# Attention weights and V multiplied in f32 on four column tiles instead of as f16 parts

## The chip, the cores and the metric

The kernel runs on one core of one Trainium2 chip. The metric is the device time of one execution in microseconds (us); less is better. The engines are PE (TensorE, with its weight loads shown as PEld), DVE (VectorE), ACT (ScalarE), POOL (GpSimd) and SP (SyncE), which issues the DMAs.

## The reference

A decoder block over 32 sequences of 128 tokens with 256 features, all in f32, cut here to its course:

```python
def mha(q_in, k_in, v_in, wq, wk, wv, wo, mask):          # 16 heads of 16 features
    q, k, v = (heads(a @ w + b) for a, w, b in ...)
    scores = einsum('bhqd,bhkd->bhqk', q, k) / 4
    scores = where(mask == 0, -1e9, scores)
    w = softmax(scores, axis=-1)
    out = einsum('bhqk,bhkd->bhqd', w, v)
    return merge(out) @ wo + bo

h0 = layernorm(x)
h1 = ln(h0 + mha(h0, h0, h0, ..., tgt_mask))              # stage A
h2 = ln(h1 + mha(h1, ctx, ctx, ..., src_mask))            # stage B
h3 = ln(h2 + relu(h2 @ w1 + b1) @ w2 + b2)                # stage C
x1 = x + tanh(g_xattn) * h3
out = x1 + tanh(g_ffn) * bitlinear_ffn(layernorm(x1))     # stage E
```

bitlinear_ffn quantizes its activations to 8 bits and its weights to three values, and is a gated network of inner width 1024.

## The kernel before

The 32 sequences go in 16 groups of two (G = 2). The five stages A, B, C, E (A and B have a part that projects, Ap and Bp) are software pipelined: in one turn of the loop, stage A works on one group, B on the group before it, and so on. The first five turns and the last ones are unrolled, the others are one hardware loop (Fori). A **unit** is one stage and one sequence; a turn has four, numbered k = 0, 1 (stage A) and 2, 3 (stage B), and -1 is the last unit of the turn before. What each engine does in a turn, and in which order, is the list SCHEDULE (lines 96 to 117), written by hand. Every engine walks through the same list and issues, in program order, its own part of each step; semaphores tie the parts together. BANK_OF (119 to 127) says which of the four PSUM banks lin_A, lin_B, lin_C and lin_E a step's result goes to.

To keep the accuracy of f32 on f16 matmuls, nearly every operand is held as two f16 tensors, a high part (the value rounded) and a low part (what is left), and a product is three matmuls: high by high, high by low, low by high (`products`, line 583). ACT writes the high part, and DVE or POOL subtracts it for the low part.

Attention of a unit goes through these steps:
- `in` and the DMAs of `parts_out`: Q and K of a group go out to DRAM (parts_AQ, ...) and come back ordered by head (stk_AQ, stk_AK, stk_BQ, stk_BK).
- `smax` (L655, L659): PE makes the scores with the queries on partitions, four heads at a time, into the bank smax. DVE takes each row's maximum (nm, L1119; L1126 and L1128 split it in two f16 parts), step `M` turns it (L669, PE), ACT copies it (mT) and a DMA puts it into two spare rows of stk_.Q.
- `scores` (L680, L685): PE makes the scores again, with the keys on partitions and the maximum already taken off, 8 heads (half a unit, hf) at a time, into the 1024 columns of st. ACT takes the exponential twice, to f32 (e32, L894) and to f16 (ehi, L896), and POOL subtracts: elo = e32 - ehi (L1283).
- `values` (lines 687 to 705): the weights are the stationary operand, V moves past them. For each of 8 heads three matmuls, of 17, 16 and 17 columns, go into the bank av, which ends with the queries on partitions. V is in vhi and vlo; vhi has a 17th column per head, a constant, which gives the sum of the weights. DVE takes the reciprocal of the sums (L1136) and multiplies (o, L1138). `values` of hf 1 is the second half.
- `O` (L714): PE turns o in two f32 transposes; ACT writes the high part oT (L905), DVE the low part (L1143).
- `W` (L593, L583): PE projects; DVE adds the residual and takes the statistics (L1150, L1037 to L1046); POOL takes the power -0.5 (lrs, L1268).
- `N`: DVE normalizes (L1051), POOL multiplies by the gain and adds the bias (L1290, L1298).

Other steps that stand around the change: `Ap` or `Bp` with `T`, `X` (transposes), `K`, `Q`, `V` (projections, each with two bias matmuls and 12 products; V's high part is written by ACT at L866, its low part vlo by DVE at L1105); `C` with `F` and `F2` (the feed forward of stage C), `stats` and `apply`; `E` with `norm` (DVE's norm and scales of the last network, then ACT at L836), `TQ` (L619), `GU` (L742), `Q2` and `DN` (L748, L752), and `setup`, once-only work on the three-valued weights in the first turns.

The order at one place of the list:

```python
    ("scores", 0, 0), ("values", -1, 1), ("Bp", "K"), ("smax", 1, 1), ("Bp", "V"), ("Bp", "T"), ("O", -1),
    ("E", "norm"), ("W", -1), ("smax", 1, 2), ("in", "B", "K"), ("N", -1), ("Bp", "Q"), ("E", "TQ"),
```

## Time and profile before

| what | value |
|---|---|
| three runs | 1305.58, 1314.23 and 1314.6 us, median 1314.23 |
| span of the profiled execution, first to last instruction | 1305.9 us (no time around it is given for this execution; its span is that of the lowest run) |
| mean granted clock of PE, of full speed | 0.880 |
| PE busy | 941.4 us (72%), 10103 matmuls |
| PEld busy (beside PE) | 737.1 us (56%) |
| DVE busy | 902.5 us (69%) |
| ACT busy | 561.7 us (43%) |
| POOL busy | 549.1 us (42%) |
| DMA | 38.2% of 16 engines' span |

How to read it: busy time counts an engine's instructions, overlaps once. A matmul's length is that of one instruction from start to end; matmuls follow each other faster than that, so what one costs in a row is the distance between starts. In rows ordered in time, a start (us from the span's start) and a length stand first, "xN" says that N instructions are merged, and the bracket is the time the engine sat idle before them and what ended it. 128*32 ahead of a shape is the part of the array that the weights fill.

### The profile page before, as it was taken

How to read it: one execution, taken by the hardware profiler on the slowest of the kernel's cores; microseconds unless marked ns; L12 is line 12 of the kernel's file. 1: busy time of each engine (PE TensorE's matmuls, PEld its weight loads, DVE VectorE, ACT ScalarE, POOL GpSimd, SP SyncE). 2: the span in 40 equal slices, each digit the busy share in tenths (PEclk: the TensorE clock that was granted, in tenths of full speed). 3: DMA queues.
4: the chain of work that ended last, by engine and by line, in shares of the span. 5: the costliest groups of instructions: out<-in, count | busy, mean ns of one | idle time of the engine just before them, and what ended most of it. 6: DMA issues, size and time to landing. Idle time of an engine off the chain costs nothing.

```text
span 1305.9 us, 28843 instructions
## 1 busy us (share of the span) xinstructions
PE 941.4 (72%) x10103; PEld 737.1 (56%) x10147; DVE 902.5 (69%) x2063; ACT 561.7 (43%) x836; POOL 549.1 (42%) x468
## 2 busy tenths in 40 slices
PE   1254567868778787878787778797878778786674
PEld 1133445646666665656665657575756666564452
DVE  8544356558787877787878788686868787666544
ACT  2212243435444554545455445453535454542432
POOL 5012134453535454444536354535453545460510
PEclk9866677979898989898999999898999898988886
DMA  4523442424444444453544425243534444404000
GB/s 139 121 81 49 78 55 42 84 40 77 64 74 75 73 73 73 57 89 53 93 53 78 64 68 75 54 81 55 86 48 76 65 65 74 66 10 66 17 9 8
DMA packets 136288, 85.07 MB, mean 65 GB/s; under 512 B 10632, under 2 KB 131631, under 8 KB 136240
## 3 DMA queue, kind: packets, MB, share of 16 engines
q1 hardware_dynamic: 136240, 84.43, 38.2%
q8 instruction: 31, 0.51, 0.2%
q14 instruction: 17, 0.14, 0.1%
...
## 4 chain that ended last, share of the span: by engine, by line
PE 27%; DVE 21%; DMA 18%; issue 16%; POOL 10%; ACT 4%; SPq 3%; DVEq 1%; POOLq 0%; ACTq 0%
DMA stk_AQ<-parts_AQ 9%; PE lin_A L583 4%; PE lin_E L583 3%; DMA parts_AQ<-qk_AQ 3%; DMA stk_BQ<-parts_BQ 3%; PE lin_B L583 3%; PE smax L659 3%; SPq L476 3%; POOL lrs L1268 2%; DVE nm_A L1119 2%; PE smax L655 2%; PE st L685 2%; DMA parts_BQ<-qk_BQ 2%; PE lin_B L752 2%; DMA stk_AQ<-mT_A 2%
## 5 line engine op out<-in xcount | busy, mean ns | idle before, releaser
L1283 POOL TENSOR_TENSOR elo<-e,ehi 128x1024 f16<-128x1024 f32 x128 | 272.6, 2130 | 303.4 <-ACT ehi L896 302.8
L894 ACT ACTIVATE e<-st 128x1024 f32<-128x1024 f32 x128 | 131.0, 1024 | 190.5 <-PE st L685 190.4
L1268 POOL TENSOR_TENSOR lrs<-lve,neghalf 128x1 f32<-128x1 f32 (+1 forms) x112 | 70.0, 625 | 333.8 <-DVE lve L1046 332.2
L1119 DVE TENSOR_REDUCE nm_A<-smax 128x4 f32<-128x512 f32 x128 | 87.8, 686 | 81.3 <-PE smax L659 80.9
L896 ACT ACTIVATE ehi<-st 128x1024 f16<-128x1024 f32 x128 | 130.9, 1022 | 0.0
L655 PE MATMUL smax<-mb,ident_big 128*128 128x512 f16 x128 | 57.6, 450 | 101.5 <-DMA stk_AQ<-parts_AQ 73.7
L1119 DVE TENSOR_REDUCE nm_B<-smax 128x4 f32<-128x512 f32 x128 | 87.7, 685 | 20.1 <-PE smax L659 19.8
L659 PE MATMUL smax<-stk_BK,stk_BQ 126*128 126x128 f16 x512 | 51.7, 225 | 45.2 <-DMA stk_BQ<-parts_BQ 40.9
L655 PEld LDWEIGHTS smax<-mb,ident_big 128*128 128x128 f16 x128 | 13.2, 103 | 112.8 <-issue 54.2
L659 PEld LDWEIGHTS smax<-stk_BK,stk_BQ 126*128 126x128 f16 x512 | 35.1, 100 | 60.3 <-issue 24.7
L875 ACT ACTIVATE late<-late,magic_col,s 128x1024 f32<-128x1024 f32 x32 | 39.7, 1240 | 60.8 <-DVE s L1195 60.8
L680 PE MATMUL st<-mbT,ident_big 128*128 128x512 f16 x128 | 54.0, 422 | 6.0 <-DMA stk_AQ<-mT_A 5.1
L659 PEld LDWEIGHTS smax<-stk_AK,stk_AQ 126*128 126x128 f16 x512 | 45.9, 110 | 21.7 <-issue 10.4
L659 PE MATMUL smax<-stk_AK,stk_AQ 126*128 126x128 f16 x512 | 57.9, 243 | 0.0
L836 ACT ACTIVATE late<-late,magic_col,s 128x256 f32<-128x256 f32 x32 | 17.5, 592 | 90.5 <-DVE kap L1080 90.5
L685 PEld LDWEIGHTS st<-stk_AQ,stk_AK 128*128 128x128 f16 x512 | 43.2, 106 | 21.3 <-issue 7.4
L685 PE MATMUL st<-stk_AQ,stk_AK 128*128 128x128 f16 x512 | 53.6, 231 | 0.0
L583 PE MATMUL lin_E<-hT_C,w 128*128 128x256 f16 x384 | 50.6, 272 | 0.0
L619 PE MATMUL lin_E<-ident,late 128*128 128x128 f32 x64 | 12.2, 321 | 51.2 <-ACT late L836 51.2
L699 PE MATMUL av<-vhi_B,ehi 128*128 128x17 f16 x512 | 45.6, 172 | 3.0 <-POOL elo L1283 3.0
L1051 DVE TENSOR_SCALAR h<-x_a,lmv,lrs 128x256 f32<-128x256 f32 x32 | 37.4, 1209 | 14.5 <-POOL lrs L1268 14.5
L685 PE MATMUL st<-stk_BQ,stk_BK 128*128 128x128 f16 x512 | 44.5, 237 | 2.6 <-DVE mw L1011 1.3
...
## 6 DMA issues: line engine op xcount, KB each, us to landing
...
```

The costliest lines, as they stand in the source:

```text
L583: mm = eng.matmul(dst, lhs(a, k), rhs(b, k), start=(start and at == 0), stop=(at == last))
L655: eng.matmul(smax[:, :], ident_big[:, :], mb[:, :].unsqueeze(1).to_broadcast([P, 4, P]), start=True, stop=True)
L659: mm = eng.matmul(smax[:, i * P:(i + 1) * P], stk[s, "Q"][0:XROW, h, tok], stk[s, "K"][0:XROW, h, tok], start=(s == "B"), stop=True, skip_ ...
L680: eng.matmul(st[:, k2 * 512:(k2 + 1) * 512], ident_big[:, :], mbT[:, :].unsqueeze(1).to_broadcast([P, 4, P]), start=True, stop=True)
L685: mm = eng.matmul(st[:, col:col + P], stk[s, "K"][:, h, tok], stk[s, "Q"][:, h, tok], start=(s == "B"), stop=True, skip_group_check=True)
L699: eng.matmul(dst, ehi[:, hf, i * P:(i + 1) * P], vhi[s][:, b, h, :], start=True, stop=False, skip_group_check=True)
L875: eng.activation(q2m[:, :], z2[:, :], ACT.Identity, scale=s2[:, 0:1], bias=magic_col[:, 0:1]).then_inc(q2_ready, 1)
L894: eng.activation(e32[:, hf, :], st[:, :], ACT.Exp, scale=SCORE).then_inc(e32_ready, 1)
L896: eng.activation(ehi[:, hf, :], st[:, :], ACT.Exp, scale=SCORE).then_inc(st_drained, 1)
L1119: eng.tensor_reduce(nm[s][:, 4 * part:4 * part + 4], smax[:, :].rearrange("p (h k) -> p h k", h=4), AX_X, ALU.max, negate=True).then_inc(s ...
L1268: eng.tensor_tensor(lrs[n][:, a:b], lve[n][:, a:b], neghalf[:, 0:b - a], ALU.pow).then_inc(ln_rstd[n], 1)
L1283: eng.tensor_tensor(elo[:, hf, :], e32[:, hf, :], ehi[:, hf, :], ALU.subtract).then_inc(elo_ready, 1)
```

## The change

V is held in one f32 tensor v32, 32 columns a head: 16 of V, and 16 of the constant. ACT writes it straight from PSUM, and DVE's subtraction is gone. The exponential is taken once, to f32 (e32); ehi, elo and POOL's subtraction are gone, and so are their semaphores. In `values` the operands change places: v32 of a head (128x32) is stationary and the weights of that head (128x128, f32) move past it. Head h = 4c + j writes partitions 32j to 32j+31 of columns 128c to 128c+127 of av: one f32 matmul a head, four heads on the four column tiles of the array. av thus holds the values with the features on partitions. ACT copies av to SBUF (av_sb) when both halves are done. A new step `R` turns av_sb back with four f32 transposes into a lin bank, and DVE's reciprocal and product read that bank. In the list, `R` of a unit stands where `O` stood or near it, `O` where `W` stood or later, and W -1, N -1, W 0 and C T move back.

```diff
-VA = DH + 1
+VA = 2 * DH
...
-    ("scores", 0, 0), ("values", -1, 1), ("Bp", "K"), ("smax", 1, 1), ("Bp", "V"), ("Bp", "T"), ("O", -1),
-    ("E", "norm"), ("W", -1), ("smax", 1, 2), ("in", "B", "K"), ("N", -1), ("Bp", "Q"), ("E", "TQ"),
...
+    ("scores", 0, 0), ("values", -1, 1), ("Bp", "K"), ("smax", 1, 1), ("Bp", "V"), ("Bp", "T"), ("R", -1),
+    ("E", "norm"), ("O", -1), ("smax", 1, 2), ("in", "B", "K"), ("Bp", "Q"), ("E", "TQ"),
...
-    plain = {"A": ("T", "K", "V"), "B": ("X", "V", "T", "Q"), "C": ("T",)}[stage]
+    plain = {"A": ("T", "K"), "B": ("X", "T", "Q"), "C": ("T",)}[stage]
...
-        vlo = {s: sb(f"vlo_{s}", [P, G, NH, DH], F16) for s in "AB"}
+        v32 = {s: sb(f"v32_{s}", [P, G, NH, VA], F32) for s in "AB"}
         nm = {s: sb(f"nm_{s}", [P, NH], F32) for s in "AB"}
         nm2 = {s: sb(f"nm2_{s}", [P, 2 * NH], F16) for s in "AB"}
         mT = {s: sb(f"mT_{s}", [2 * NH, P], F16) for s in "AB"}
         e32 = sb("e32", [P, 2, 1024], F32)
-        ehi = sb("ehi", [P, 2, 1024], F16)
-        elo = sb("elo", [P, 2, 1024], F16)
+        av_sb = sb("av_sb", [P, 512], F32)
         rsum = sb("rsum", [P, NH], F32)
         o = {s: sb(f"o_{s}", [P, NH, DH], F32) for s in "AB"}
...
                 for i in range(8):
                     h = 8 * hf + i
-                    dst = av[:, h * VA:h * VA + VA]
-                    eng.matmul(dst, ehi[:, hf, i * P:(i + 1) * P], vhi[s][:, b, h, :], start=True, stop=False,
-                               skip_group_check=True)
-                    eng.matmul(av[:, h * VA:h * VA + DH], ehi[:, hf, i * P:(i + 1) * P], vlo[s][:, b, h, :],
-                               start=False, stop=False, skip_group_check=True)
-                    mm = eng.matmul(dst, elo[:, hf, i * P:(i + 1) * P], vhi[s][:, b, h, :], start=False, stop=True,
-                                    skip_group_check=True)
+                    c, j = h // 4, h % 4
+                    mm = eng.matmul(av[VA * j:VA * (j + 1), c * P:(c + 1) * P], v32[s][:, b, h, :],
+                                    e32[:, hf, i * P:(i + 1) * P], start=True, stop=True)
                 mm.then_inc(av_filled, 1)
+
+            def rows_back(st_, k):
+
+                s, b, g, turn = st_.unit(k)
+                bank, fill, drain, before, after = st_.job(s, ("R", k))
+                wait(eng, drain, before)
+                eng.wait_ge(av_drained, turn.at(1, 1))
+                for c in range(4):
+                    mm = eng.transpose(bank[:, c * P:(c + 1) * P], av_sb[:, c * P:(c + 1) * P], ident[:, :])
+                mm.then_inc(fill, 1)
 
             def output_rows(st_, k):
 
...
+                eng.wait_ge(*st_.read(s, ("R", k)))
                 for c in range(DC):
                     mm = eng.transpose(bank[:, c * P:(c + 1) * P],
...
                 elif name == "V":
-                    dst = vhi[s][:, :, :, 0:DH].rearrange("p b h d -> p (b h) d")
+                    dst = v32[s][:, :, :, 0:DH].rearrange("p b h d -> p (b h) d")
                     src = bank[:, :].rearrange("p (n d) -> p n d", d=DH)
+                    eng.activation(dst, src, func).then_inc(drain, 1)
+                    return
...
                 if what == "scores":
                     eng.wait_ge(st_filled, turn.at(2, hf + 1))
-                    wait(eng, elo_ready, turn.at(2, hf - 1))
-                    eng.activation(e32[:, hf, :], st[:, :], ACT.Exp, scale=SCORE).then_inc(e32_ready, 1)
                     wait(eng, av_filled, turn.at(2, hf - 1))
-                    eng.activation(ehi[:, hf, :], st[:, :], ACT.Exp, scale=SCORE).then_inc(st_drained, 1)
+                    eng.activation(e32[:, hf, :], st[:, :], ACT.Exp, scale=SCORE).then_inc(st_drained, 1)
+                elif what == "values":
+                    if hf == 0:
+                        return
+                    eng.wait_ge(av_filled, turn.at(2, 2))
+                    wait(eng, sums_ready, turn.at(1))
+                    eng.activation(av_sb[:, :], av[:, :], ACT.Copy).then_inc(av_drained, 1)
                 elif what == "M":
...
-                    i_ = eng.tensor_tensor(vlo[s][:, :, :, :].rearrange("p b h d -> p (b h) d"),
-                                           bank[:, :].rearrange("p (n d) -> p n d", d=DH),
-                                           vhi[s][:, :, :, 0:DH].rearrange("p b h d -> p (b h) d"), ALU.subtract)
                 else:
...
                     eng.scalar_tensor_tensor(nm2[s][:, NH:2 * NH], nm[s][:, :], 1.0 / MS, nm2[s][:, 0:NH], ALU.mult,
                                              ALU.subtract).then_inc(max_ready[s], 1)
-                elif what == "values":
-
-                    if part == 0:
-                        return
-                    eng.wait_ge(av_filled, turn.at(2, 2))
-                    heads = av[:, 0:NH * VA].rearrange("p (h v) -> p h v", v=VA)
+                elif what == "R":
+
+                    bank, fill, drain, before, after = st_.job(s, ("R", k))
+                    eng.wait_ge(fill, after)
+                    heads = bank[:, :].rearrange("p (h v) -> p h v", v=VA)
                     eng.reciprocal(rsum[:, :], heads[:, :, DH]).then_inc(sums_ready, 1)
                     eng.wait_ge(sums_ready, turn.at(1, 1))
                     eng.tensor_tensor(o[s][:, :, :], heads[:, :, 0:DH], rsum[:, :].unsqueeze(2).to_broadcast([P, NH, DH]),
-                                      ALU.mult).then_inc(av_drained, 1)
+                                      ALU.mult).then_inc(drain, 1)
                 elif what == "O":
...
 
-                const(eng.memset(vhi[s][:, :, :, DH:VA].rearrange("p b h o -> p (b h o)"), WS))
+                const(eng.memset(v32[s][:, :, :, DH:VA].rearrange("p b h o -> p (b h) o"), WS))
             assert n_const[0] == N_CONST
...
             def unit_step(st_, what, k, hf=0):
                 s, b, g, turn = st_.unit(k)
                 n = LN_OF[s]
-                if what == "scores":
-                    eng.wait_ge(st_drained, turn.at(2, hf + 1))
-                    wait(eng, av_filled, turn.at(2, hf - 1))
-                    eng.tensor_tensor(elo[:, hf, :], e32[:, hf, :], ehi[:, hf, :], ALU.subtract).then_inc(elo_ready, 1)
-                elif what == "W":
```

The steps as PE issues them, at the turn's start, behind V and T of stage B: lin_E<-ident,o_B is O -1, brows and w_BO are W -1, w_BQ is Bp Q. Before:

```order
L583 MATMUL lin_C<-w_BV,hT_B 128x256 x12
L613 MATMUL lin_A<-ident,h 128x128 x4
L714 MATMUL lin_E<-ident,o_B 128x128 x2
L593 MATMUL lin_E<-brows,ones 128x256
L583 MATMUL lin_E<-w_BO,oT_B 128x256 x6
L655 MATMUL smax<-mb,ident_big 128x512
L659 MATMUL smax<-stk_AK,stk_AQ 128x128 x4
L591 MATMUL lin_B<-ones,brows 128x256
L583 MATMUL lin_B<-hT_B,w_BQ 128x256 x6
```

The same place on PE, now:

```order
L581 MATMUL lin_C<-w_BV,hT_B 128x256 x12
L611 MATMUL lin_A<-ident,h 128x128 x4
L708 MATMUL lin_B<-ident,av_sb 128x128 x4
L718 MATMUL lin_E<-ident,o_B 128x128 x2
L653 MATMUL smax<-mb,ident_big 128x512
L657 MATMUL smax<-stk_AK,stk_AQ 128x128 x4
L589 MATMUL lin_B<-ones,brows 128x256
L581 MATMUL lin_B<-hT_B,w_BQ 128x256 x6
...
L591 MATMUL lin_E<-brows,ones 128x256
L581 MATMUL lin_E<-w_BO,oT_B 128x256 x6
```

R -1 (av_sb) has come in, directly ahead of O -1, and W -1 has moved behind B's Q and two smax steps.

Further on, still on PE, where stage A's K and Q are projected: brows with w_AO is W 0, nm_B is M 2, w_AK and w_AQ are the projections. Before:

```order
L703 MATMUL av<-vhi_A,elo 128x17
L593 MATMUL lin_E<-brows,ones 128x256
L583 MATMUL lin_E<-w_AO,oT_A 128x256 x6
L669 MATMUL lin_C<-ident,nm_B 32x128
L659 MATMUL smax<-stk_BK,stk_BQ 128x128 x4
L591 MATMUL lin_A<-ones,brows 128x256
L583 MATMUL lin_A<-hT_A,w_AK 128x256 x6
```

The same place on PE, now:

```order
L718 MATMUL lin_C<-ident,o_A 128x128 x2
L667 MATMUL lin_C<-ident,nm_B 32x128
L657 MATMUL smax<-stk_BK,stk_BQ 128x128 x4
L589 MATMUL lin_A<-ones,brows 128x256
L581 MATMUL lin_A<-hT_A,w_AK 128x256 x6
...
L581 MATMUL lin_B<-hT_A,w_AQ 128x256 x6
L591 MATMUL lin_E<-brows,ones 128x256
L581 MATMUL lin_E<-w_AO,oT_A 128x256 x6
```

W 0 stood ahead of K and Q and stands behind them now; O 0 is where W 0 was.

On DVE, at the turn's start ahead of stage E's norm (lst<-late): rsum and o_B are the reciprocal and product, oT_B is O -1's low part. Before:

```order
L1119 TENSOR_REDUCE nm_A<-smax 128x4
L1136 RECIPROCAL rsum<-av 128x16
L1138 TENSOR_TENSOR o_B<-av,rsum 128x256
L1099 TENSOR_TENSOR qf_B<-lin_A,anyb 128x512
L1119 TENSOR_REDUCE nm_A<-smax 128x4
L1105 TENSOR_TENSOR vlo_B<-lin_C,vhi_B 128x512
L1090 TENSOR_TENSOR hT_B<-lin_A,hT_B 128x512
L1143 TENSOR_TENSOR oT_B<-lin_E,oT_B 128x256
L1037 BN_STATS lst<-late 128x6 x2
```

The same place on DVE, now:

```order
L1131 TENSOR_REDUCE nm_A<-smax 128x4
L1115 TENSOR_TENSOR qf_B<-lin_A,anyb 128x512
L1131 TENSOR_REDUCE nm_A<-smax 128x4
L1106 TENSOR_TENSOR hT_B<-lin_A,hT_B 128x512
L1147 RECIPROCAL rsum<-lin_B 128x16
L1149 TENSOR_TENSOR o_B<-lin_B,rsum 128x256
L1051 BN_STATS lst<-late 128x6 x2
```

The reciprocal and product have moved behind hT_B's low part, vlo_B is gone, and oT_B's low part comes after stage E's norm.

## Rows read from the trace of the kernel before

**Rows 1.** Stretches: us, then PE, PEld, DVE, ACT, POOL busy; clock, DMA, GB/s

```profile
0.00:300.00 300.00, 157.45 (x1503) 118.21 (x1505) 166.42 (x316) 86.56 (x123) 99.64 (x87) 0.77 0.40 77
300.00:1100.00 800.00, 646.48 (x7347) 516.42 (x7382) 615.82 (x1453) 395.23 (x596) 380.86 (x321) 0.93 0.43 69
...
800.00:813.60 13.60, 13.55 (x167) 11.45 (x166) 11.75 (x32) 9.13 (x13) 7.19 (x7) 1.00 0.65 91
744.30:813.60 69.30, 55.03 (x628) 43.40 (x631) 53.99 (x126) 33.86 (x51) 33.09 (x29) 0.95 0.43 69
```

**Rows 2.** PE in order of time: start us, length us, engine, line

```profile
749.26 0.60 PE L655 MATMUL smax<-mb,ident_big 128*128 128x512 f16 x1 [4.71 <-DMA stk_AQ<-parts_AQ]
...
753.25 0.38 PE L655 MATMUL smax<-mb,ident_big 128*128 128x512 f16 x1
```

**Rows 3.** The chain that ended last, from 800 us on: start, length

```profile
806.15 2.87 DMA parts_AQ<-qk_AQ
...
810.38 8.28 DMA stk_AQ<-parts_AQ
```

**Rows 4.** PE's waits from 744.3 to 813.6: us in total, times, longest

```profile
PE smax L655 <- DMA stk_AQ<-parts_AQ: 4.7, 1, 4.7
PE lin_E L619 <- ACT late L836: 2.5, 1, 2.5
PE lin_E L593 <- DVE oT_B L1143: 1.8, 1, 1.8
PE smax L655 <- DVE nm_A L1119: 1.7, 1, 1.7
PE smax L659 <- DMA stk_BQ<-parts_BQ: 1.2, 1, 1.2
PE lin_C L669 <- DVE nm_A L1128: 1.1, 1, 1.1
```

**Rows 5.** PE in order of time: a values block, and around L669

```profile
743.52 0.18 PE L699 MATMUL av<-vhi_B,ehi 128*128 128x17 f16 x1
...
744.14 0.42 PE L714 MATMUL lin_A<-ident,o_A 128*128 128x128 f32 x2
...
812.74 0.23 PE L669 MATMUL lin_B<-ident,nm_B 128*32 128x128 f16 x1
812.90 0.18 PE L699 MATMUL av<-vhi_B,ehi 128*128 128x17 f16 x1
```

**Rows 6.** PE in order of time, the set-up and the first projection

```profile
24.58 2.08 PE L554 MATMUL lin_E<-late,bvb 128*128 128x256 f32 x4
...
44.64 1.49 PE L583 MATMUL lin_A<-hT_A,w_AK 128*128 128x256 f16 x6
```

**Rows 7.** PE in order of time, f32 transposes and f16 scores

```profile
803.71 0.62 PE L748 MATMUL lin_A<-ident,late 128*128 128x128 f32 x4
804.20 0.66 PE L748 MATMUL lin_B<-ident,late 128*128 128x128 f32 x4
...
805.24 0.61 PE L685 MATMUL st<-stk_BQ,stk_BK 128*128 128x128 f16 x8
```

**Rows 8.** Groups: busy us, mean ns of one, idle before and its end

```profile
L1283 POOL TENSOR_TENSOR elo<-e,ehi 128x1024 f16<-128x1024 f32 x128 | 272.6, 2130 | 303.4 <-ACT ehi L896 302.8
L896 ACT ACTIVATE ehi<-st 128x1024 f16<-128x1024 f32 x128 | 130.9, 1022 | 0.0
L1051 DVE TENSOR_SCALAR h<-x_a,lmv,lrs 128x256 f32<-128x256 f32 x32 | 37.4, 1209 | 14.5 <-POOL lrs L1268 14.5
L1051 DVE TENSOR_SCALAR late<-late,lmv,lrs 128x256 f32<-128x256 f32 x64 | 29.9, 509 | 14.2 <-POOL lrs L1268 14.2
L1138 DVE TENSOR_TENSOR o_B<-av,rsum 128x256 f32<-128x256 f32 x32 | 13.6, 425 | 1.1
```

**Rows 9.** DVE and POOL in order of time, one place

```profile
759.86 1.59 DVE L1126 TENSOR_SCALAR nm_A<-nm_A 128x16 f16<-128x16 f32 x1
...
759.30 2.12 POOL L1283 TENSOR_TENSOR elo<-e,ehi 128x1024 f16<-128x1024 f32 x1
```

More of the change, by code:

```diff
@@ L105 @@
     ("scores", 1, 0), ("smax", 2, 1), ("E", "GU", 0, 3), ("values", 0, 1), ("E", "GU", 1, 0), ("smax", 2, 2),
[2 rows of a table removed]
[2 rows of a table added]
     ("setup", 0), ("E", "GU", 1, 2), ("E", "DN", 0, 0), ("E", "DN", 0, 1), ("N", 0), ("E", "GU", 1, 3),
     ("scores", 2, 0), ("smax", 3, 2), ("values", 1, 1), ("in", "A", "Q"), ("E", "Q2", 1), ("setup", 1),
[1 row of a table removed]
[1 row of a table added]
     ("C", "stats"), ("O", 1), ("smax", 4, 0), ("E", "DN", 0, 2), ("setup", 2), ("W", 1),
-    ("scores", 3, 0), ("smax", 4, 1), ("values", 2, 1), ("N", 1), ("E", "DN", 1, 0), ("smax", 4, 2),
[1 row of a table added]
     ("E", "DN", 1, 1), ("O", 2), ("scores", 3, 1), ("smax", 4, 3), ("E", "DN", 1, 2), ("W", 2), ("M", 4),
@@ L159, in job_of @@
         return None
-    if step[0] in ("M", "O", "W"):
+    if step[0] in ("M", "R", "O", "W"):
         return unit_of(t, step[1])[0], step
@@ L711, in output_rows @@
                 wait(eng, drain, before)
-                eng.wait_ge(av_drained, turn.at(1, 1))
+                eng.wait_ge(*st_.read(s, ("R", k)))
                 for c in range(DC):
@@ L914, in iteration @@
                         continue
-                    if what in ("scores", "M", "O"):
+                    if what in ("scores", "values", "M", "O"):
                         unit_step(st_, *step)
+                    elif what in ("R",):
+                        continue
                     elif name in ("GU", "DN", "Q2"):
@@ L1212, in iteration @@
                         continue
-                    if what in ("smax", "values", "O", "W", "N"):
+                    if what in ("smax", "R", "O", "W", "N"):
                         unit_step(st_, *step)
+                    elif what == "values":
+                        continue
                     elif step == ("Ap", "norm"):
```

13 lines of the change are left out of this document (8 added, 5 removed), and 9 rows, old and new, of the table SCHEDULE.

## Prediction

> **What bounds the kernel now.** I read the page first (its busy shares are in the table above: TensorE, PE, 72%, VectorE, DVE, 69%, nothing full), then the table of stretches, PE's waits, the groups, and last the rows in order of time. The stretches [rows 1] show that the page's average mixes two kinds of time: PE is busy 157 of the first 300 us (filling the pipeline, once-only weight work), but 646 of the 800 us from 300 to 1100, which is the loop; the last 206 us drain it. PE waits for stk_AQ at 749.26 [rows 2], and the next turn's load of it lands at 810.38 + 8.28 = 818.7 [rows 3], so a turn takes about 69.3 us and the middle holds 800 / 69.3 = 11.5 of them. The list of PE's waits in the turn from 744.3 to 813.6 [rows 4] has 4.7 + 2.5 + 1.8 + 1.7 + 1.2 + 1.1 = 13.0 us, and smaller ones of 1.0. PE is thus occupied 69.3 - 14.0 = 55.3 us; it is the fullest engine, and it waits for the answers of other engines to its own results: a chain through DRAM, and layer norms on DVE and GpSimd (POOL). More PE work is paid for in full outside such a chain and costs nothing beside one. So I work out a turn from both: PE's work, and each wait anew.
>
> **The values step carries the answer.** Before, half a unit is 24 f16 matmuls of 17 or 16 columns: the first starts at 743.52, the next step (L714) at 744.14 [rows 5], 0.62 us. There are 128 such blocks, 8 a turn. After, a block is 8 f32 matmuls that move 128 columns, each into its own quarter of the output partitions.
>
> What an f32 matmul costs, the set-up shows. L554 issues two of 256 columns, and the row has four instructions in 2.08 us [rows 6]: two per matmul, (2.08 - 0.63) / 3 = 0.48 apart, 0.63 being the length of one. The f16 matmuls of 256 columns at 44.64 are about (1.49 - 0.42) / 5 = 0.21 apart [rows 6]. Where the granted clock is 1.00 [rows 1], a f16 matmul of 128 columns takes (0.61 - 0.23) / 7 = 0.054 us [rows 7], a quarter of 0.21 for half the columns. The early rows thus ran at the lower of the two levels, and there an f32 instruction cost about two f16 passes, an f32 matmul four. At the upper level a new matmul is 4 x 0.054 = 0.22 us, and eight in a row are 1.74 us. What the four column tiles can do side by side no row shows: the one matmul on a narrow tile, L669 (128*32), always stands alone.
>
> The bounds are 1.74 / 4 = 0.44 us, all tiles at once, and 1.74, none beside another. I take a value between: the two instructions of a matmul use one tile, so the second cannot stream while the first does, and if instructions start in order, only the second of one head overlaps the first of the next. The queue then moves on by 0.11 a matmul: 8 x 0.11 + 0.11 = 1.0 us.
>
> To this comes a change of tile size at both ends. After L669 at 812.74 the next matmul starts 0.16 later [rows 5], not 0.054: 0.1 us. Taken twice a block, 0.2 (nothing, if that gap was a wait). The block becomes 1.2 us, +0.58, with ends +0.02 (no overlap lost, with the changes) and +1.3.
>
> The Trainium skill, page TensorEngine Tiling (Array Packing), Key Properties, says that different tiles can load weights and multiply in parallel, but that changing the tiling mode drains the engine. By its first half the block would be the 0.44 us of full overlap, by its second that change is owed at every block, which speaks against the edit; the 0.16 us behind L669 agrees with the second half, and no run here shows the first.
>
> **The other parts, per turn of four units.**
> - R, four f32 transposes a unit. L748 has the shape: one set of four starts at 803.71, the next at 804.20 [rows 7], some 0.45 each. +1.8 us.
> - ScalarE (ACT) loses L896, 1.02 us x 8 [rows 8], and gains one 128x512 f32 copy a unit, between nothing seen and that 1.02. It was busy 33.9 of 69.3 [rows 1], so nothing comes of it by itself.
> - POOL loses elo, 2.13 us x 8 [rows 8]. It stood in front of the values, but is not among PE's waits [rows 4]: the old order hides it already.
> - DVE loses vlo and gains more in another way. While elo runs, DVE's tensor_scalar from SBUF to SBUF stands still: L1126, 16 columns, takes 1.59 us at 759.86, beside an elo from 759.30 to 761.42 [rows 9]. L1051 writing h averages 1.21 us, the same shape writing late 0.51 [rows 8]; 0.7 x 2 a turn, L1126 twice, and the nrm groups between: about 3 us of DVE a turn. Worth nothing where DVE is not waited for, all 3 at most.
> - Clock: behind the wait of 4.7 us L655 takes 0.60 instead of the 0.38 it takes four us later [rows 2], so some 4 us of PE work run at the lower level and cost 2. A wait half as long gives back about 1.
>
> PE's work: 55.3 + 8 x 0.58 + 1.8 - 1.0 = 60.7 us.
>
> **Each wait anew [rows 4].**
> - stk_AQ, 4.7: its chain (DVE, ACT, POOL, DMAs of 2.87 and 8.28 [rows 3]) stays. PE's work beside it grows by two blocks (1.2), R 1 (0.45) and W 0, which now follows Q instead of preceding K (seven matmuls of 256 columns, 14 x 0.054 = 0.76). 2.3 are left.
> - oT_B, 1.8, ahead of W -1: goes with W's move, but O -1 now follows R -1 at once and needs DVE's reciprocal and product (L1138 0.42 [rows 8], about 0.7 together), behind hT_B's low part. Queued behind O -1 on PE are smax and B's Q. 2.1.
> - ACT late L836, 2.5: PE comes to it as before (O -1 starts where W -1 did), but DVE starts that norm behind o_B instead of oT_B, 0.4 later. 2.9.
> - nm_A, 1.7 + 1.1: L1126's stall sits in it. 1.2.
> - stk_BQ, 1.2: W -1 and a block are now beside it. 0.
> - The small ones 1.0, and 0.6 for R 2, which has only four transposes between it and O 2.
> Sum 10.1; 60.7 + 10.1 = 70.8. Of DVE's 3 us I count 1.2 on the way, the part in the norms that PE waits for: 69.6 us a turn, against 69.3. Over 11.5 turns +4 us. At both ends PE is half idle and units run by their latency. There a half unit loses 1.02 + 2.13 us ahead of its values and gains up to 1.3: I take 8 us less in all, of 0 to 20. For the profiled execution that is 1305.9 + 4 - 8 = 1302 us. Of the three runs before, one (1305.6) is at its span and two are at 1314, with 8 us more at the median; I add half of that: **1306 us**, about no change (this measurement tells some 1% from none).
>
> **Rivals.**
> 1. *The tiles do not overlap* (slower). Block 1.74 + 0.2 = 1.9 us, +1.3. PE: 55.3 + 10.4 + 1.8 - 1.5 = 66.0; waits: stk_AQ 0.9, the rest as above, 8.7; less 1.2: 73.5. +4.2 x 11.5 - 4 = +44: 1350, and +10 at the ends, where passes at the lower level take twice as long: 1360. It decides from a block of 1.3 us up. For it: two instructions per matmul, and no row with an overlap. Against it: no row excludes one.
> 2. *Four tiles at once* (faster). Block 0.64; PE 55.3 + 0.2 + 1.8 - 0.3 = 57.0; waits 3.5 + 2.1 + 2.9 + 1.2 + 0.4 + 1.6 = 11.7; less 1.2: 67.5. -1.8 x 11.5 - 10 = -31: 1278. For it: the four heads of a group share nothing. Against it: both instructions of a head on one tile.
> 3. *Each change from one tile to another costs the 0.1 us of L669*, not only the change of size: 8 x (0.22 + 0.1) = 2.6 us a block, +2.0, 16 us of PE a turn. Some 7 fall into waits: +9 x 11.5 = 104: 1415.
> 4. *DVE's relief counts in full*, with the middle block: 1.8 us a turn more, 21 us, and 10 more at the ends: 1275. For it: L1126 and L1051 are in chains that PE waits for. Against it: DVE waits for PE as well.
>
> **How the numbers follow.** Middle case 0.35 (own range 1290 to 1325: faster by over 1% 0.08, within 0.22, slower 0.05), no overlap 0.25 (slower), four at once 0.21 (faster 0.18, same 0.03), full relief 0.13 (faster), a price per tile 0.06 (slower). Faster 0.39, same 0.25, slower 0.36. The range leaves out the last case and the outer ends of the others: 1262 to 1378.
>
> **What would show it.** In the changed kernel's profile: from the first values matmul to the next step's first 1.2 us (rivals 0.64, 1.9, 2.6), and a head's second instruction starting with the next head's first. L1051 on h near 0.5 us. PE's wait for stk_AQ near 2.3. A turn of 69.6 us. A block over 1.3 us with a turn of 69 or less would prove my reading of the waits wrong; a block of 1.2 and a turn near 67, the value I put on DVE's relief.

## The result, and the profile after it

| | before | changed kernel |
|---|---|---|
| median of four runs each | 1314.41 us | 1423.24 us (1419.59 to 1432.34) |
| span of the profiled execution | 1305.9 us | 1417.8 us |
| mean granted clock of PE | 0.880 | 0.862 |

The ratio is 1.089, with a 95% interval from 1.085 to 1.093. The forecast was 1306 us, about no change, the range 1262 to 1378. The measured time lies well above the range.

The head of the page of the changed kernel: busy time, its share of the span, the number of instructions.

```profile
span 1417.8 us, 26952 instructions
PE 1004.4 (71%) x9379; PEld 747.7 (53%) x9379; DVE 829.0 (58%) x2031; ACT 490.6 (35%) x772; POOL 280.7 (20%) x340
```

DVE has 73 us less to do than before, ACT 71 and POOL 268, and the kernel is 109 us slower. So it didn't become slower by work on those three. PE is busy 63 us longer, with fewer matmuls.

The stretches of the changed kernel, with columns as in [rows 1]; the last is one turn.

```profile
300.00:1100.00 800.00, 619.24 (x6048) 469.93 (x6046) 497.01 (x1266) 307.15 (x489) 165.99 (x204) 0.90 0.37 61
...
497.00:574.90 77.90, 60.68 (x581) 45.62 (x579) 48.01 (x123) 29.31 (x47) 16.32 (x20) 0.89 0.38 61
```

A turn was 69.3 us and is 77.9. That is 8.6 us, and over 11.5 turns 99 of the 109 us: the loss is in the loop. PE is busy 60.7 us of it (55.0 before) at a clock of 0.89 (0.95 before). Both are single turns. From the starts of M 2 in the traces, ten or eleven turns of the middle have these means, which later comparisons use:

| | a turn | PE busy | PE idle | granted clock |
|---|---|---|---|---|
| before | 68.6 us | 55.3 | 13.4 | 0.94 |
| changed kernel | 77.2 us | 59.6 | 17.5 | 0.90 |
| changed kernel in the old order (below) | 68.2 us | 57.6 | 10.6 | 0.93 |

PE's waits in that turn of the changed kernel, with columns as in [rows 4].

```profile
PE lin_C L667 <- DVE oT_A L1154: 4.6, 1, 4.6
PE lin_E L617 <- DVE oT_B L1154: 3.9, 1, 3.9
PE lin_B L611 <- POOL h L1307: 2.9, 1, 2.9
PE smax L653 <- DMA stk_AQ<-parts_AQ: 1.7, 1, 1.7
PE lin_E L718 <- DVE o_B L1149: 1.7, 1, 1.7
PE lin_E L591 <- DVE late L1196: 1.0, 1, 1.0
```

With three smaller ones of 1.4 us in all the list sums to 17.2 us, against 14.0. The wait for stk_AQ has shrunk from 4.7 to 1.7, as foreseen, and stk_BQ's is gone. But three lines have no counterpart before: M 2 (L667, nm_B into bank C) waits 4.6 us for oT_A, C T (L611) 2.9 us for h, and W 0 (L591, the last row) 1.0 us: it now stands behind GU 1 1 and fills the same bank E, which DVE has yet to read (L1196). The forecast had none of them. TQ (L617) waits 3.9 where it waited 2.5.

The values step in the changed kernel, PE in order of time.

```profile
502.96 0.39 PE L683 MATMUL st<-stk_AQ,stk_AK 128*128 128x128 f16 x4
503.28 0.64 PE L697 MATMUL av<-e,v_B 128*32 128x128 f32 x16
503.86 0.28 PE L589 MATMUL lin_A<-ones,brows 128*128 128x256 f16 x1
```

A block takes 503.86 - 503.28 = 0.58 us, changes of tile size included; over the 124 blocks with all sixteen records the median is 0.58. It was 0.62 before [rows 5], and the forecast was 1.2. The sixteen instructions of this block (two per matmul, as in [rows 6]) start at these times, in ns from the first:

```
0 7 13 20 | 133 140 147 153 | 242 249 256 262 | 352 358 365 372
```

Four start together and four more every 0.11 us, which is the time of one f32 instruction of 128 columns at the upper level. So four column tiles seem to work at once; the records don't name a tile, and a run below tests it.

Four groups of the changed kernel, with columns as in [rows 8].

```profile
L697 PE MATMUL av<-e,v_B 128*32 128x128 f32 x1024 | 41.5, 280 | 0.0
L908 ACT ACTIVATE av_sb<-av 128x512 f32<-128x512 f32 x64 | 38.0, 594 | 11.7 <-PE av L697 11.6
L1065 DVE TENSOR_SCALAR h<-x_a,lmv,lrs 128x256 f32<-128x256 f32 x32 | 11.8, 410 | 14.5 <-POOL lrs L1281 14.5
L1138 DVE TENSOR_SCALAR nm_A<-nm_A 128x16 f16<-128x16 f32 x32 | 5.6, 175 | 3.2
```

ACT's copy takes 0.59 us. The norm's product on h fell from 1.21 us [rows 8] to 0.41, and nm_A's scaling, which took 1.59 beside elo [rows 9], averages 0.18. The arithmetic does what it was meant to.

**Why M 2 waits.** All engines from 540 us on, in order of time. O 0 is L718 on PE, L917 on ACT (high part), L1154 on DVE (low part).

```profile
541.03 0.44 PE L718 MATMUL lin_C<-ident,o_A 128*128 128x128 f32 x2
...
542.00 1.21 DVE L1200 TENSOR_REDUCE am<-late 128x1 f32<-128x1024 f32 x1
...
543.94 1.24 ACT L883 ACTIVATE late<-late,magic_col,s 128x1024 f32<-128x1024 f32 x1 [2.57 <-DVE s L1206]
545.08 0.36 ACT L917 ACTIVATE oT_A<-lin_C 128x256 f16<-128x256 f32 x1
545.48 0.42 DVE L1154 TENSOR_TENSOR oT_A<-lin_C,oT_A 128x256 f16<-128x256 f32 x1 [1.45 <-ACT oT_A L917]
546.03 0.28 PE L667 MATMUL lin_C<-ident,nm_B 128*32 128x128 f16 x1 [4.56 <-DVE oT_A L1154]
```

O 0 fills bank C by 541.5. M 2 needs nothing of O 0, but it is the next step in the list and writes the same bank. The bank is read out first by ACT, in whose order Q2's rounding (L883) stands ahead. L883 waits 2.57 us for the scale that DVE is still finding. Then ACT reads, then DVE, and PE starts 4.56 us late. Before, five steps stood between O 0 and M 2.

**Why TQ waits**: the same form, in bank E with O -1. ACT's read of it stands behind stage E's own scaling.

```profile
514.18 1.09 ACT L842 ACTIVATE late<-late,magic_col,s 128x256 f32<-128x256 f32 x2 [5.75 <-DVE kap L1094]
515.18 0.36 ACT L917 ACTIVATE oT_B<-lin_E 128x256 f16<-128x256 f32 x1
...
515.57 0.42 DVE L1154 TENSOR_TENSOR oT_B<-lin_E,oT_B 128x256 f16<-128x256 f32 x1 [1.50 <-ACT oT_B L917]
...
516.12 1.11 PE L617 MATMUL lin_E<-ident,late 128*128 128x128 f32 x4 [3.88 <-DVE oT_B L1154]
```

Here most of the wait was owed anyway: L842, TQ's own input, ends at 515.27. The bank adds 516.12 - 515.27 = 0.85 us.

**Why C T waits.** Again all engines; W -1 ends with res_B, and nrm_B, tg_B and h are the layer norm behind it (N -1), whose result C T turns.

```profile
519.64 0.42 DVE L1161 SCALAR_TENSOR_TENSOR res_B<-lin_E,hres_B 128x256 f32<-128x256 f32 x1 [0.30 <-PE lin_E L581]
...
523.33 0.41 DVE L1065 TENSOR_SCALAR nrm_B<-res_B,lmv,lrs 128x256 f32<-128x256 f32 x1
...
523.82 0.72 POOL L1299 TENSOR_TENSOR tg_B<-nrm_B,lng 128x256 f32<-128x256 f32 x1 [2.26 <-DVE nrm_B L1065]
...
524.70 0.72 POOL L1307 TENSOR_TENSOR h<-tg_B,lnb 128x256 f32<-128x256 f32 x1 [0.17 <-POOL tg_B L1299]
525.48 0.88 PE L611 MATMUL lin_B<-ident,h 128*128 128x128 f32 x3 [2.91 <-POOL h L1307]
```

From res_B to h are 525.42 - 519.64 = 5.8 us, of which 3.3 pass before nrm_B starts on DVE, behind the norm's statistics, POOL's root and GU's products. PE has only three small GU steps, some 2.5 us, to lay beside that. Before, two smax steps, Bp Q, TQ and two GU steps stood between W -1 and C T.

### The profile page after: what moved, and what is told of

It is laid out like the page before. It is cut to its first block, busy times and chain, and to the rows that moved or that the text cites. A ratio compares the mean times of both kernels' runs of the same rounds, so it can differ in the third digit from the quotient of the medians.

```text
span 1417.8 us, 26952 instructions
## 1 busy us (share of the span) xinstructions
PE 1004.4 (71%) x9379; PEld 747.7 (53%) x9379; DVE 829.0 (58%) x2031; ACT 490.6 (35%) x772; POOL 280.7 (20%) x340
## 4 chain that ended last, share of the span: by engine, by line
PE 44%; DVE 17%; DMA 13%; issue 12%; POOL 6%; ACT 6%; SPq 2%; DVEq 0%; POOLq 0%; ACTq 0%
DMA stk_AQ<-parts_AQ 8%; PE lin_A L581 6%; PE lin_E L581 6%; PE lin_B L581 5%; DMA parts_AQ<-qk_AQ 3%; PE smax L657 3%; PE av L697 3%; PE st L683 3%; PE smax L653 2%; PE st L678 2%; DVE am L1200 1%; SPq L474 1%; POOL qk_AQ L1287 1%; POOL lrs L1281 1%; PE lin_B L756 1%
## 5 line engine op out<-in xcount | busy, mean ns | idle before, releaser
L1287 POOL TENSOR_TENSOR qk_AQ<-qf_A,qk_AQ 128x512 f16<-128x512 f32 x16 | 18.5, 1154 | 352.2 <-ACT qk_AQ L857 352.2
L617 PE MATMUL lin_E<-ident,late 128*128 128x128 f32 x64 | 16.2, 403 | 73.2 <-DVE oT_B L1154 62.0
L883 ACT ACTIVATE late<-late,magic_col,s 128x1024 f32<-128x1024 f32 x32 | 39.7, 1240 | 74.4 <-DVE s L1206 74.4
L678 PE MATMUL st<-mbT,ident_big 128*128 128x512 f16 x128 | 55.3, 432 | 3.5 <-DMA stk_AQ<-mT_A 3.5
L683 PE MATMUL st<-stk_AQ,stk_AK 128*128 128x128 f16 x512 | 56.5, 240 | 0.0
L842 ACT ACTIVATE late<-late,magic_col,s 128x256 f32<-128x256 f32 x32 | 17.5, 593 | 100.3 <-DVE kap L1094 100.3
L617 PEld LDWEIGHTS lin_E<-ident,late 128*128 128x128 f32 x64 | 10.1, 195 | 77.5 <-ACT late L842 45.7
L611 PE MATMUL lin_B<-ident,h 128*128 128x128 f32 x64 | 13.1, 340 | 53.4 <-POOL h L1307 53.4
L667 PE MATMUL lin_C<-ident,nm_B 128*32 128x128 f16 x16 | 4.3, 268 | 62.9 <-DVE oT_A L1154 60.7
L697 PE MATMUL av<-e,v_A 128*32 128x128 f32 x1024 | 47.4, 307 | 0.0
L581 PE MATMUL lin_A<-w,late 128*128 128x256 f16 x384 | 44.9, 274 | 0.0
```

Of the source, the lines that this page charges most:

```text
L581: mm = eng.matmul(dst, lhs(a, k), rhs(b, k), start=(start and at == 0), stop=(at == last))
L617: mm = eng.transpose(bank[:, at:at + P], q1m[:, b, c * P:(c + 1) * P], ident[:, :])
L678: eng.matmul(st[:, k2 * 512:(k2 + 1) * 512], ident_big[:, :], mbT[:, :].unsqueeze(1).to_broadcast([P, 4, P]), start=True, stop=True)
L683: mm = eng.matmul(st[:, col:col + P], stk[s, "K"][:, h, tok], stk[s, "Q"][:, h, tok], start=(s == "B"), stop=True, skip_group_check=True)
L697: mm = eng.matmul(av[VA * j:VA * (j + 1), c * P:(c + 1) * P], v32[s][:, b, h, :], e32[:, hf, i * P:(i + 1) * P], start=True, stop=True)
L883: eng.activation(q2m[:, :], z2[:, :], ACT.Identity, scale=s2[:, 0:1], bias=magic_col[:, 0:1]).then_inc(q2_ready, 1)
```

## The experiments

My theory after reading the trace (ORDER in the expectations): the loss comes from where the steps stand and which bank they use, and the new arithmetic is a gain. Against it stood readings in which the new arithmetic, through the f32 matmuls or R, is what costs. All runs have the kernel before on the same chip beside them; ratios are to it, with 95% intervals, and I compare kernels of different chips by their ratios only (the kernel before had medians of 1314.9, 1314.7 and 1309.0 us on the three chips). Where waits, busy or idle times of whole runs are given, they are those of one profiled execution each.

**One bank.** M 2 goes to bank E.

```diff
-("B", ("M", 2)): "C"
+("B", ("M", 2)): "E"
```

> The changed kernel, with M 2 in bank E instead of C, so that it does not wait until O 0's result in bank C is read. Theory ORDER (the loss comes from where steps stand and which bank they share): PE's wait of 4.6 us ahead of M 2 goes, and with it some lower clock, 3 to 5 us a turn of 77.9: about 1380 us, 1365 to 1395. Theory LENGTH (the loss comes from the longer way of a unit: copy, R, reciprocal, O, W, and from R's work on PE): the wait only moves, 1410 or more.

1349.86 us, 1.028 (1.022 to 1.033). One letter is worth 5.6% (1.028 / 1.089), 73 us. PE's waits, whole run:

```profile
PE lin_E L617 <- DVE oT_B L1154: 61.8, 15, 7.8
PE lin_B L611 <- POOL h L1307: 55.3, 16, 5.3
...
PE lin_E L667 <- DVE nm_B L1140: 11.5, 16, 2.1
```

In the changed kernel L667's wait in bank C was 60.7 us over 15 turns; here it is 11.5, for its own input. That is 49 us less of this wait, but 73 less of time. Not all of the 49 is gained: W 0's wait for DVE in bank E grows from 13.1 to 26.6 us. PE's idle time falls by 38 us in all (413.4 to 375.3). PE's busy time falls by 29 (1004.4 to 975.6) with the same matmuls: between 300 and 1100 us the granted clock is 0.94 instead of 0.90. The expectation had 3 to 5 us a turn for wait and clock together; by the mean turn it was 5.5 (77.2 to 71.7), and the time came out below its range.

**Both banks.** Besides, O -1 goes from bank E to C, away from TQ.

```diff
-("B", ("O", -1)): "E"
+("B", ("O", -1)): "C"
```

> The changed kernel with M 2 in bank E and O -1 in bank C, so that stage E's TQ in bank E does not wait for O -1's low part, which DVE makes behind the whole norm. ORDER: besides M 2's wait that of TQ falls from 3.9 to about 2.7 us: 1365 us, 1350 to 1385. LENGTH: 1400 or more.

1346.60 us, 1.026 (1.020 to 1.032): not told apart from the last, and a little below the range. TQ's wait is again for ACT's L842 and not for the bank, as the 0.85 us above allow, and little more than that was to be had.

**The order alone, in the kernel before.** Its list gets the changed kernel's order (R left out of it), its arithmetic stays.

```diff
-("Bp", "T"), ("O", -1), ("E", "norm"), ("W", -1), ("smax", 1, 2), ("in", "B", "K"), ("N", -1), ...
+("Bp", "T"), ("E", "norm"), ("O", -1), ("smax", 1, 2), ("in", "B", "K"), ("Bp", "Q"), ("E", "TQ"),
+("smax", 1, 3), ("in", "B", "Q"), ("W", -1), ..., ("N", -1), ("E", "GU", 0, 2), ("C", "T"),
...
-("C", ("F", 3)), ("O", 0), ("scores", 1, 1), ..., ("values", 1, 0), ("W", 0), ("M", 2)
+("C", ("F", 3)), ("scores", 1, 1), ..., ("values", 1, 0), ("O", 0), ("M", 2), ..., ("W", 0)
```

> The kernel before (f16 parts, elo, no R) with the changed kernel's order: O -1 behind the norm, O 0 ahead of M 2, W -1, N -1, C T and W 0 later, banks as they are. ORDER: it takes over the waits for oT_A ahead of M 2, for oT_B ahead of TQ and for h ahead of C T, 4 to 7 us a turn more than 69.3: 1365 to 1400. LENGTH: 1314 to 1325, since the way of a unit is short here.

1448.13 us, 1.102 (1.096 to 1.108): more than the whole change costs, and more than the 1365 to 1400 expected. Its three largest waits, whole run:

```profile
PE lin_E L619 <- DVE oT_B L1143: 72.2, 15, 7.7
PE lin_C L669 <- DVE oT_A L1143: 59.9, 15, 4.5
PE lin_B L613 <- POOL h L1298: 54.5, 16, 5.3
```

They are the changed kernel's three, in a kernel that has neither R nor an f32 values step.

**The arithmetic alone.** The changed kernel in the old order, with R as early as its input allows (R -1 behind Bp K, R 0 behind GU 1 0; R 2 too stands one smax step earlier than in the changed kernel, other than the expectation says).

```diff
-("Bp", "K"), ("smax", 1, 1), ("Bp", "V"), ("Bp", "T"), ("R", -1), ("E", "norm"), ("O", -1),
+("Bp", "K"), ("R", -1), ("smax", 1, 1), ("Bp", "V"), ("Bp", "T"), ("O", -1), ("E", "norm"), ("W", -1),
...
-("R", 0), ("scores", 1, 1), ("smax", 2, 3), ("E", "Q2", 0), ("values", 1, 0), ("O", 0), ("M", 2)
+("O", 0), ("scores", 1, 1), ("smax", 2, 3), ("E", "Q2", 0), ("values", 1, 0), ("W", 0), ("M", 2)
```

> The changed kernel with the order of the kernel before: O, W, N and C T where they stood, and R put between values and O (R -1 behind K, R 0 behind GU 1 0, R 1 and R 2 as in the changed kernel). ORDER: a turn of 67 to 70 us, 1285 to 1325. LENGTH: waits ahead of R and O take the place of the ones that go, 1390 or more.

1288.99 us, 0.982 (0.977 to 0.988). One turn's waits:

```profile
PE smax L653 <- DMA stk_AQ<-parts_AQ: 4.1, 1, 4.1
PE lin_E L617 <- ACT late L842: 2.5, 1, 2.5
PE lin_E L591 <- DVE oT_B L1154: 1.7, 1, 1.7
PE smax L657 <- DMA stk_BQ<-parts_BQ: 1.5, 1, 1.5
```

Three more are 0.3 each. These are the old kernel's waits [rows 4] without the ones for nm_A. Little of the gain is in the loop: the mean turn is 68.2 us against 68.6, with PE busy 2.3 us longer and idle 2.8 less. Of the 18.6 us between the two spans, some 14 lie outside the eleven middle turns, where the pipeline fills and drains. The two orders and the two arithmetics together:

| | f16 values, elo | f32 values, R |
|---|---|---|
| old order | 1 | 0.982 |
| new order | 1.102 | 1.089 |

The arithmetic gains 1.2 to 1.8% in either order, and the order loses 10 to 11% with either arithmetic (with the new one, R's places are part of the order). That settles the main question. The rest takes the order and the arithmetic apart, from the kernel with the old order ("the base" below).

**O 0 directly ahead of M 2** (and W 0 behind GU 1 1), nothing else of the new order.

```diff
-("C", ("F", 3)), ("O", 0), ..., ("values", 1, 0), ("W", 0), ("M", 2), ..., ("E", "GU", 1, 1)
+("C", ("F", 3)), ..., ("values", 1, 0), ("O", 0), ("M", 2), ..., ("E", "GU", 1, 1), ("W", 0)
```

> e5_old_order with the changed kernel's places of O 0 and W 0 alone: O 0 directly ahead of M 2, both in bank C, W 0 behind GU 1 1. Theory ORDER: M 2 waits until ACT and DVE have read O 0, 4.5 us a turn, and the kernel loses what e1_m2_bank gained: 1289 + 55 to 80 = 1345 to 1370 us. If that loss needed the rest of the changed order: below 1320.

1336.81 us, 1.020 (1.013 to 1.027), 3.8% over the base, less than the 1345 to 1370 expected. The wait is there again:

```profile
PE lin_C L667 <- DVE oT_A L1154: 58.4, 15, 4.4
```

W 0's wait behind GU 1 1 comes with it (13.1 us), and the wait for stk_AQ falls from 64.3 us in the base to 33.1 (W 0's move alone brings 21 of that in the next run). PE's idle time grows by 32 us in all, its busy time by 16.

**W 0 late, O 0 where it was.** W 0 goes behind A's K and Q, but ahead of GU 1 1, and into bank C.

```diff
-("values", 1, 0), ("W", 0), ("M", 2), ("smax", 3, 0), ("Ap", "K"), ("Ap", "Q"), ("in", "A", "K"),
+("values", 1, 0), ("M", 2), ("smax", 3, 0), ("Ap", "K"), ("Ap", "Q"), ("in", "A", "K"), ("W", 0),
```

> e5_old_order with W 0 behind the projections of Q (as the changed kernel has it), but in bank C, where it meets nobody. PE's wait for stk_AQ (3.8 us a turn) should shrink by the 0.76 us of W 0, which no longer stands ahead of K and Q: 1278 to 1284 us. If res_A of unit 0 then comes late for N 0, no gain: 1286 or more.

1282.48 us, 0.980 (0.972 to 0.988). The total wait for stk_AQ falls from 64.3 us in the base to 43.3, while M 2 now waits 16.2 for its own input. Moving W 0 back does no harm in this place and bank; behind GU 1 1 in bank E, where the changed kernel has it, it waits the 13.1 us named above. This is the fastest kernel of the study, though not told apart from the base.

**W -1, N -1 and C T late**, nothing else of the new order.

```diff
-("E", "norm"), ("W", -1), ("smax", 1, 2), ("in", "B", "K"), ("N", -1), ("Bp", "Q"), ("E", "TQ"),
-("smax", 1, 3), ("in", "B", "Q"), ("E", "GU", 0, 0), ("E", "GU", 0, 1), ("C", "T"), ("E", "GU", 0, 2),
+("E", "norm"), ("smax", 1, 2), ("in", "B", "K"), ("Bp", "Q"), ("E", "TQ"),
+("smax", 1, 3), ("in", "B", "Q"), ("W", -1), ..., ("N", -1), ("E", "GU", 0, 2), ("C", "T"),
```

> e5_old_order with the changed kernel's places of W -1, N -1 and C T alone; R -1 and O -1 stay early. ORDER, by this part: the 1.67 us that PE waits ahead of W -1 go, but C T comes 2.9 to 3.3 us before h is there and the chain behind N -1 starts some 5 us later: 1289 + 15 to 40. If the loss at the turn's start is all from R -1 and O -1 around the norm: 1270 to 1290.

1370.01 us, 1.047 (1.039 to 1.055), 6.6% over the base and twice what was expected. Its largest waits, whole run:

```profile
PE lin_E L617 <- ACT late L842: 75.7, 16, 11.2
PE smax L653 <- DMA stk_AQ<-parts_AQ: 62.9, 15, 8.7
PE lin_B L611 <- POOL h L1307: 52.8, 16, 5.3
```

C T's wait for h is new with 52.8 us; TQ's is 75.7 where the base has 51.2, because W -1 no longer stands in front of it as work; the wait of W -1 for oT_B (26.0 in the base) is gone, and stk_BQ's falls from 36.0 to 9.8. B's Q now waits 14.0 for hT_B. With small ones PE's idle time grows by 42 us and its busy time by 38, the granted clock of the middle being 0.90 where the base has 0.93: together the 80 us between the two spans. C T late has a tail too, which the chain that ended last shows:

```profile
660.86 0.72 POOL h L1307
661.58 3.26 issue
...
664.88 0.72 POOL lrs L1281
...
666.02 0.42 DVE h L1065
...
666.59 0.39 SPq L504
...
667.10 2.49 DMA stk_AQ<-mT_A
...
669.71 0.39 PE st L678
```

In the stretch called issue DVE takes hT_C's low part, C T's result, at 662.96 and only then stage A's norm, from 663.57; SP's queue holds the load of x_a (L504) until that norm is done, and the maxima's load for the next scores is queued behind it. No run takes this tail away alone.

**The whole turn start of the changed kernel**: also R -1 behind Bp T and O -1 behind stage E's norm.

```diff
-("Bp", "K"), ("R", -1), ("smax", 1, 1), ("Bp", "V"), ("Bp", "T"), ("O", -1), ("E", "norm"),
+("Bp", "K"), ("smax", 1, 1), ("Bp", "V"), ("Bp", "T"), ("R", -1), ("E", "norm"), ("O", -1),
```

> e5_old_order with the changed kernel's whole turn start: R -1 behind T, O -1 behind the norm, and W -1, N -1, C T late. With e10_o0_m2 (+48 us over e5 for the other half of the order) and the changed kernel at 1423, ORDER expects the remaining 1423 - 1337 = 86 us here, if the halves add up: 1350 to 1380. If they share a cover: 1320 to 1345.

1389.09 us, 1.060 (1.053 to 1.066), 7.9% over the base, 1.2% over the last, and a little above the expected range. O -1 right behind R -1 waits 26.9 us in all for o_B (DVE), as in the changed kernel. The two halves, 7.9% here and 3.8% with O 0, give 1.079 x 1.038 = 1.120, where the changed kernel stands at 1.089 / 0.982 = 1.109 of the base. The new order's loss is accounted for, with a little overlap.

**W -1 and N -1 between Bp Q and TQ**, on top of the fastest, with W -1 in bank C, to see whether a smaller step back is free.

```diff
-("E", "norm"), ("W", -1), ("smax", 1, 2), ("in", "B", "K"), ("N", -1), ("Bp", "Q"), ("E", "TQ"),
+("E", "norm"), ("smax", 1, 2), ("in", "B", "K"), ("Bp", "Q"), ("W", -1), ("N", -1), ("E", "TQ"),
```

> e9_w0_late with W -1 and N -1 between B's Q and TQ, W -1 in bank C. PE's wait of 1.67 us ahead of W -1 is covered by Q, and W -1 itself stands in the 2.5 us that PE waits ahead of TQ: up to 1.67 us a turn less, 1262 to 1275 us. If N -1's result then comes late for C T: 1278 or more.

1294.90 us, 0.987 (0.980 to 0.994): no gain over the fastest (0.980, 0.972 to 0.988), from which it is not told apart, and so a miss. TQ's wait is 62.4 us where the kernel it starts from has 51.1, and C T waits 31.6 for h again. I had looked at the wait that goes (oT_B) and not at the chain that starts later, the prediction's mistake once more.

**Four heads in a row on one tile.** The base with head and tile numbered the other way; the same matmuls, and DVE reads the bank accordingly.

```diff
-                    c, j = h // 4, h % 4
+                    c, j = h % 4, h // 4
```

> e5_old_order with the heads spread so that four heads in a row use the same column tile (DVE reads R's bank in the order that goes with it; same matmuls, same results). If the 0.58 us block of the changed kernel comes from four tiles that run at once, the block becomes 8 x 0.22 = 1.74 us, and the turn grows by 8 x 1.2 = 9.6 us less what fits into PE's waits for stk_AQ (3.8) and stk_BQ (1.5): 1330 to 1380 us. If the block is short for another reason, it stays near 0.6 and the time at 1289.

1334.05 us, 1.017 (1.011 to 1.024), 3.6% over the base. PE in order of time:

```profile
543.28 0.23 PE L667 MATMUL lin_B<-ident,nm_B 128*32 128x128 f16 x1
543.35 1.50 PE L697 MATMUL av<-e,v_B 128*32 128x128 f32 x16
544.78 0.44 PE L718 MATMUL lin_A<-ident,o_A 128*128 128x128 f32 x2
```

A block is now 1.46 us at the median, so the overlap across tiles is worth 0.88 us a block, 113 us of PE over 128 blocks. Only about 46 us are paid. PE's busy time grows by 90 us, its idle time falls by 44, and the granted clock from 300 to 1100 us is 0.97 instead of 0.93. The first row also settles a doubt of the prediction: between L667 and the values matmuls, both on narrow tiles, the starts are 0.07 us apart here, against 0.16 behind L669 [rows 5], where the next matmul is on the whole array. So most of that gap was the change of tile size.

The starts (ns) form two chains of eight, the first of each chain followed after 133, the others 109 or 110 apart. So it is, within 2 ns, in 91 of the 124 blocks. In most of the others, like the one shown, which follows L667 at once, the first step is 110 and the form is the same.

```
0 133 242 352 461 570 679 788
467 600 709 818 927 1037 1146 1255
```

The records don't name the tile, but two instructions 6 ns apart, at 461 and 467, can't be on the same one. So the second tile's first instruction starts while three of the first tile's eight have yet to start. If the program's order of heads is also the order of the instructions, PE doesn't keep to it between tiles; the records alone don't show which instruction belongs to which head.

**R's transposes issued twice**, on the base; the second set writes the same values again.

```diff
-                for c in range(4):
+                for c in (0, 1, 2, 3, 0, 1, 2, 3):
```

> e5_old_order with R's four transposes issued twice, the second time over the first (same result). It prices the part that the change adds to PE: +0.45 us x 4 = 1.8 us a turn, 21 us over 11.5 turns and some at the ends. Paid in full: 1289 + 20 to 28. If PE's waits take most of it: 1289 + 0 to 12.

1305.05 us, 0.996 (0.993 to 1.000; ten runs), 1.4% over the base, 18 us, close to the 11.5 x 1.8 = 21 us of extra PE work in the loop. But the two profiled executions, one of each kernel, don't show it there. The mean turn grows from 68.2 to 68.6 us only, PE busy 1.2 us longer and idle 0.8 less, at a granted clock of 0.95 instead of 0.93. Some 11 of the 16 us between the two spans lie outside the middle turns. So a second R costs about 0.4 us a turn in the loop, where PE's waits and the clock take up most of it, and is paid for where the pipeline fills and drains. That the total matches the sum is luck.

**POOL busy as with elo.** The base plus one POOL subtraction of elo's size for each half unit, at elo's place, into a tensor that nothing reads.

```diff
+                if what == "scores":
+                    eng.wait_ge(st_drained, turn.at(2, hf + 1))
+                    wait(eng, spare_done, turn.at(2, hf))
+                    eng.tensor_tensor(spare[:, :, :], ones[:, :].unsqueeze(1).to_broadcast([P, 8, P]),
+                                      ones16[:, 0:P].unsqueeze(1).to_broadcast([P, 8, P]), ALU.subtract).then_inc(spare_done, 1)
```

> e5_old_order plus one POOL operation of elo's size per half unit, into a spare tensor (ones minus ones16), which nothing waits for. It takes back what POOL's freedom gives: DVE's tensor_scalar stands still beside it again. Theory RELIEF (e5 is faster than the kernel before because DVE no longer stalls): 1289 + 15 to 30 us, up to the 1314 of before. Theory LATENCY (the gain is the shorter way from the scores to the values and the block): +0 to 8 us.

1375.84 us, 1.052 (1.044 to 1.060), 7.1% over the base, far above the expectation. The groups:

```profile
L1298 POOL TENSOR_TENSOR spare<-ones 128x1024 f16<-128x1024 f32 x128 | 272.5, 2129 | 277.7 <-ACT e L904 274.1 <-issue 3.4
L1067 DVE TENSOR_SCALAR h<-x_a,lmv,lrs 128x256 f32<-128x256 f32 x32 | 37.4, 1208 | 14.5 <-POOL lrs L1283 14.5
L1140 DVE TENSOR_SCALAR nm_A<-nm_A 128x16 f16<-128x16 f32 x32 | 33.8, 1055 | 3.2
```

DVE's products on h are back at 1.21 us, and nm_A's scaling is at 1.06 where the changed kernel has 0.18. No engine reads the spare tensor, so what this costs is what POOL's presence costs: DVE's stalls, and POOL's own norms queued behind. PE's idle time grows by 72 us, and 50 of them stand ahead of the M steps: PE's waits there for nm_A and nm_B are 57.3 us in the whole run, against 7.2 in the base. That is the path on which the stalled scaling lies.

It isn't the price of elo. The kernel before has the real elo, and these waits are 19.0 us in it; the spare operation starts behind the one exponential that is left (L904), elo started behind the second (L896). If the spare operation stood for elo, this kernel should lie above the kernel before by what R costs, 1.4% for its transposes; it lies 5.2% above. So elo's own price is open. What the base shows is a net: 1.8% gained in spite of R, so the new arithmetic relieves some 3%, and more if R's longer way (copy, transposes, reciprocal) costs anything beyond its transposes, which no run prices.

## Why the prediction was wrong, step by step

- **"Each wait anew" is the step that failed.** I treated the moves of W 0 and W -1 as cover for waits and asked for every wait of before how long it would be. I didn't ask which new ones would arise. Three did, and two carry the loss. *M 2 behind O 0*: priced at nothing, 4.6 us a turn, worth 5.6% by the bank alone and, with W 0's new place, 3.8% put into the base. The rows of the order stood in my own text (o_A into lin_C, then nm_B into lin_C), and I never read the bank in them. *C T behind N -1*: priced at nothing, 2.9 us a turn; with TQ's and the lower clock 6.6%. *W 0 behind GU 1 1*: priced as a gain for stk_AQ, and it waits 1.0 us in bank E. From the base to the changed kernel the mean turn grows by 9.0 us, 7.0 of idle time and 2.0 of matmuls that run slower.
- **O -1 behind R -1**: 2.1 us forecast, 1.7 measured. Right.
- **TQ**: 2.9 forecast, 3.9 measured. I had it starting later behind o_B; the bank shared with O -1 adds 0.85.
- **stk_AQ**: 2.3 forecast, 1.7 measured; **stk_BQ** 0 and 0. Right: PE does lay its new work beside the DMAs. **nm_A**: 1.2 forecast and absent from the turn shown. Sum of waits: 10.1 forecast, 17.2 measured.
- **The values block**: +0.58 us forecast, -0.04 measured. The f32 price (0.11 us an instruction, two a matmul) and the 0.1 at each change of tile size were sound: four times 0.11, and 0.1 at each end, are 0.64. What failed is the premise that instructions start in order. Rival 2, four tiles at once, was true of the block (0.64 forecast, 0.58 measured) and had a chance of 0.21. That its time, 1278 us, is close to the 1289 of the run with the old order is luck: its waits were worked out for the new order.
- **R**, +1.8 us a turn: about right as PE's work, but I took it as paid in full. A second R added 0.4 us to the mean turn and some 11 us outside the middle turns.
- **DVE's relief**: in the loop about right. I took 1.6 us a turn off nm_A's waits and 1.2 more for the relief, 2.8 together. In the turn shown of the base the waits for nm_A (2.8) are gone, and PE's mean idle time is 2.8 us less than before. How the gain splits between DVE's stalls and the shorter way to the values no run tells.
- **Ends**, 8 us less of 0 to 20: right for the arithmetic (some 14 less in the base outside the middle turns), wrong for the changed kernel (some 18 more), where the new waits stand in those turns too.
- **Clock**, +1 us a turn given back: wrong sign. The wait for stk_AQ did shrink, but with the new waits the granted clock is 0.90 in the middle, and PE is busy 59.6 us of a mean turn instead of the base's 57.6. How much of a loss comes this way is no fixed rate: one bank took 38 us off PE's idle time and 29 off its busy time, O 0 ahead of M 2 added 32 and 16, the spare operation on POOL 72 and 9.
- The test I had set, "a block over 1.3 us with a turn of 69 or less would prove my reading of the waits wrong", was one-sided. A block of 0.58 with a turn of 77.9 proves it as well.
